# Splitting the negated row maxima of a two-layer cross-attention on GpSimd instead of VectorE

## The chip, the core and the metric

The kernel runs on one core of one Trainium2 chip. The metric is the time of one execution on the device in microseconds. TensorE multiplies matrices, VectorE and ScalarE work on tiles in SBUF and PSUM, GpSimd works on tiles in SBUF, and SyncE issues the DMAs. Each engine takes its own instructions in order; semaphores join them.

## The reference

Two cross-attention layers over 4 batches of 1024 tokens, 16 heads each, all in float32. Layer 0 (heads of 64) is a layer norm, projections of `h = layernorm(x)` and of the context, then

```python
attn = jnp.einsum('bihd,bjhd->bhij', Q, K)
attn = jax.nn.softmax(attn, axis=-1) * scale
vals = jnp.einsum('bhij,bjhd->bihd', attn, V).reshape(B, NQ, INNER)
x = x + vals @ Wo + bo
```

Its scores are not scaled ahead of the softmax, so the kernel subtracts a maximum of each row. Layer 1 (heads of 32) is an RMS norm, a rotary embedding and an L2 normalisation of q and k, a softmax over bounded logits (no maximum is needed), and again a projection and a residual.

## The kernel before, in words

A **turn** is a batch, a layer and a group of heads: two heads of 64 in layer 0 (8 turns a batch), four of 32 in layer 1 (4 turns). A turn has two halves of 512 query tokens. `PLAN` is a list of steps, 4 for a half of layer 0 and 8 for one of layer 1. A step of layer 0 makes the scores of two key tiles of 128, their exponentials (ScalarE), the running sum of the exponentials (VectorE, `added`, L904) and the product with the values (TensorE, `attend`, L721). Beside that it does other work that the plan lists by hand (`layer0_beside`, `layer1_beside`): projections of the next turns, output projections, and the row maxima of layer-0 halves to come. All engines walk the same plan through `run` (L532), each with its own order inside a step; VectorE uses `on_vector` (L268), the others the default of `run`.

**The row maxima.** For a half, TensorE makes eight tiles of plain scores (`rowmax` of TensorE, L668), in two banks of `work`, the only three-bank PSUM buffer for everything beside the attention. VectorE reduces each to one negated maximum per row and head (L883, `tile_max`), which frees the banks. After the eighth, always the last tile maximum of step 1 of a layer-0 half, or of a step in the last layer-1 turn, VectorE takes the minimum over the two halves of the keys (L887, `neg`, 128x8), copies it to bfloat16 (L889) and subtracts that copy from the float32 value for a second bfloat16 part (L891). The two parts lie in `neg_max` in columns 0, 64 and 1, 65 of each tile. There are 64 such completions in the run. Entry `T`, in the next step, has TensorE multiply `neg_max` by an identity (L769) to turn the parts into rows; ScalarE copies them to `shift` (L847), which joins the scores as a fourth product with ones.

**Around it in a steady half of layer 0.** Behind L891 VectorE makes `q_low` or `k_low` (L978, from PSUM and SBUF), normalises the last half's output (`o_sum`, L910, both inputs in SBUF, waits for a DMA of `recip`), reduces the first tile maximum of step 2 (L883) and adds the step's two exponentials (L904, both inputs in SBUF). On TensorE L721 is followed by an output projection (`out`, L793), which claims one of the banks that the tile maximum reads, and then by `T`.

**GpSimd** does the rest of the rotary work for each `kr` and `qr` entry (`finish_rotation`: a power L1028, an addition L1030, a multiplication L1033), the inverse root of the norms (L1049), and the bias addition (L1041, after a DMA of `resid`). Turn 7 of a batch, first half, has `kr` of turn 8 in step 1 and again in step 2; it is the only completion of row maxima whose step has such an entry. In `on_vector` the last tile maximum of a step stands ahead of the step's last entry if that is a `q`, `k`, `kT` or `qT`, and behind all entries if not, so behind this `kr`. VectorE's part of `kr` is five operations ending with L969.

Of the kernel before, what the change touches and what calls it, by code (L numbers as in the profile page):

```python
# [10 lines left out]
ALU = mybir.AluOpType  # L11
ACT = mybir.ActivationFunctionType
AX = mybir.AxisListType

B, S, D, DC = 4, 1024, 512, 384
P = 128
TT = S // P
HALF = 512
HT = HALF // P
XC, CC = D // P, DC // P  # L20
HEADS = 16
D0, D1 = 64, D // HEADS
G0, G1 = P // D0, P // D1
# [347 lines left out]
def max_no(t, n):  # L371

    b, _, p = TURN[t]
    return b * 2 * TURNS0 + ORDER.index((p, n)) + 1


def norm_no(which, half):
    b, l = which
    return 4 * b + 2 * l + half + 1


def build(nc, rows, x, ctx_in, wq0, wk0, wv0, wo0, bo, gamma, beta, norm_w, wq1, wkv1, wout1,
# [16 lines left out]
    def tiles_of(half):  # L399
        return slice(half * HT, (half + 1) * HT)  # L400

    with ExitStack() as ctx:
        def sb(name, shape, dt=F32, scope=ctx):
            return scope.enter_context(nc.sbuf_tensor(name, shape, dt))

        def sem(name):
            return ctx.enter_context(nc.semaphore(name))
# [30 lines left out]
        den_t = sb("den_t", [P, G1, HT])  # L438
        recip_t = sb("recip_t", [P, G1, HT])
        tile_max = sb("tile_max", [P, HT, G0, 2])  # L440
        neg = sb("neg", [P, HT, G0])
        neg_max = sb("neg_max", [P, HT, P], BF16)
        ident_b = sb("ident_b", [P, P], BF16)
        shift = [sb(f"shift{i}", [P, S], BF16) for i in range(2)]
# [21 lines left out]
        consts_ok = sem("consts_ok")  # L466
# [14 lines left out]
        act_freed = sem("act_freed")  # L481
        dve_freed = sem("dve_freed")
        high_ok = sem("high_ok")
        neg_step = sem("neg_step")
        neg_max_ok = sem("neg_max_ok")
        scores_ok = sem("scores_ok")
# [41 lines left out]
        def maxima_banks(e):  # L528

            return work[:, 0:2, :] if e.banks[0] < BANKS else scores[:, e.banks[0] - BANKS:e.banks[1] - BANKS + 1, :]  # L530

        def run(rowmax, scored, blocks, entry, order=lambda st: (st.first + st.early, st.fill + st.rest)):  # L532

            for at, st in enumerate(PLAN):
                after = PLAN[at + 1] if at + 1 < len(PLAN) else None
                if after is not None and not st.late:
                    for kt in after.kts:
                        scored(after.t, after.n, kt)
                ahead, beside = order(st)
                for e in ahead:  # L540
                    (rowmax if e.kind == "R" else entry)(e)
                for kt in st.kts:
                    blocks(st.t, st.n, kt)
                for e in beside:
                    (rowmax if e.kind == "R" else entry)(e)
                if after is not None and st.late:
                    for kt in after.kts:
                        scored(after.t, after.n, kt)
# [328 lines left out]
        def _(dve):  # L877
            def rowmax(e):
                half, n, qt = e.i
                if (n, qt) == (0, 0) and (e.t, half) != (0, 0):  # L880
                    dve.wait_ge(neg_max_ok, max_no(e.t, half) - 1)
                dve.wait_ge(work_full, e.full)
                dve.tensor_reduce(tile_max[:, qt, :, n:n + 1], maxima_banks(e), AX.X, ALU.max, negate=True).then_inc(dve_freed, 1)  # L883
                if (n, qt) == (1, HT - 1):
                    dve.wait_ge(dve_freed, e.dve)
                    no = 2 * max_no(e.t, half)
                    dve.tensor_reduce(neg[:, :, :], tile_max[:, :, :, :], AX.X, ALU.min).then_inc(neg_step, 1)  # L887
                    dve.wait_ge(neg_step, no - 1)
                    dve.tensor_copy(neg_max[:, :, 0:D0 + 1:D0], neg[:, :, :]).then_inc(neg_step, 1)  # L889
                    dve.wait_ge(neg_step, no)  # L890
                    dve.tensor_tensor(neg_max[:, :, 1:D0 + 2:D0], neg[:, :, :], neg_max[:, :, 0:D0 + 1:D0], ALU.subtract).then_inc(neg_max_ok, 1)  # L891

            def added(t, n, kt):
                if kt == 0 or kt > last_sum(t):
# [123 lines left out]
            dve.wait_ge(ident_in, 16)  # L1018
            dve.tensor_copy(ident_b[:, :], ident[:, :]).then_inc(consts_ok, 1)
            run(rowmax, lambda t, n, kt: None, added, entry, on_vector)  # L1020

        @block.gpsimd
        def _(pool):
            def finish_rotation(e):
                which, no, ts = "kq".index(e.kind[0]), e.rope, tiles_of(e.i)
                vec = raw[which][:, ts, :, :]
                pool.wait_ge(sumsq_ok, no)
                pool.tensor_tensor(inv[no % 2][:, :], sumsq[no % 2][:, :], power[:, :], ALU.pow).then_inc(turn_step, 1)  # L1028
                pool.wait_ge(dve_freed, e.dve)
                pool.tensor_tensor(vec, vec, turned[no % 2][:, :, :, :], ALU.add).then_inc(turn_step, 1)  # L1030
                pool.wait_ge(turn_step, 2 * no)
                vec = vec.rearrange("p t h d -> p (t h) d")
                pool.tensor_tensor(vec, vec, inv[no % 2][:, :].unsqueeze(2).broadcast_to([P, HT * G1, D1]), ALU.mult).then_inc(scaled_ok, 1)  # L1033

            def add_bias(b, half):
                ts = tiles_of(half)
                if b == 0:
                    pool.wait_ge(bias_in, 16)
                    pool.wait_ge(xn_ok, norm_no((0, 0), 1))
                pool.wait_ge(resid_in[half], 16 * (b + 1))  # L1040
                pool.tensor_tensor(resid[:, ts, :], resid[:, ts, :], bo_all[:, :].unsqueeze(1).broadcast_to([P, HT, D]), ALU.add).then_inc(bias_ok, 1)  # L1041

            def entry(e):
                if e.kind in ("kr", "qr"):
                    finish_rotation(e)
                elif e.kind == "norm_a":
                    ts = tiles_of(e.i)
                    pool.wait_ge(var_ok, norm_no(e.t, e.i))
                    pool.tensor_tensor(rstd[:, ts], var_eps[:, ts], power[:, 0:HT], ALU.pow).then_inc(rstd_ok, 1)  # L1049
                elif e.kind == "add_bias":  # L1050
                    add_bias(e.t, e.i)
                elif e.kind == "swap":
                    add_bias(e.t, e.i)

            pool.memset(power[:, :], -0.5).then_inc(power_ok, 1)
            pool.wait_ge(power_ok, 1)
            run(lambda e: None, lambda t, n, kt: None, lambda t, n, kt: None, entry)


# [37 lines left out]
```

## Time and profile before

| | us |
|---|---|
| median of three runs | 3179.01 |
| lowest, highest | 3171.63, 3180.96 |
| the profiled execution, its own time | 3179.22 |
| its span, first to last instruction | 3177.4 |
| granted TensorE clock, mean | 0.996 |

The profiled execution has its time beside its span: the instructions fill 3177.4 us of 3179.22. In the timeline a row is one instruction or several of the same line merged: start, duration (of all merged), engine, line, operation, what it writes and reads, and the count; in brackets the idle time of its engine ahead of it and what ended it. PEld is the weight load of TensorE, which can run ahead of the matmul that needs it. The ends of matmuls are modelled, so distances between starts are safer than ends.

### The profile page before, as it was taken

The page shows a single profiled execution, that of the slowest core. Times are in us where ns is not written, and L with a number is a line of the kernel's source. Part 1 is how long each engine was busy: PE and PEld are TensorE (multiplying, and loading weights), DVE is VectorE, ACT ScalarE, POOL GpSimd, SP SyncE. Part 2 cuts the span into 40 slices and gives each one's busy share as a digit, 9 for nine tenths or more (in the row PEclk, how much of TensorE's full clock was granted, in tenths as well). Part 3 has the DMA queues.
Part 4 walks back from the last instruction along what each step waited for, and adds up shares of the span by engine and source line. Part 5 has one row for each costly group of instructions (what it writes and reads, how often), then busy time and mean ns, then how long its engine had stood idle before and what let it go on. Part 6 is the DMA issues. An engine that isn't in the chain of part 4 may idle for free.

```text
span 3177.4 us, 70528 instructions
## 1 busy us (share of the span) xinstructions
PE 3042.6 (96%) x30408; PEld 1482.9 (47%) x30408; DVE 2297.7 (72%) x2683; ACT 1395.4 (44%) x1497; POOL 488.0 (15%) x221
## 2 busy tenths in 40 slices
PE   7999998999999999999999999999999999999998
PEld 4444445554444444555444444455534444445553
DVE  5777777787677777678667777768866777776867
ACT  3333333556433333356643333335563333334565
POOL 1000003450000000245000000125401000013540
PEclk9999999999999999999999999999999999999999
DMA  3000100211210101020121010102112010100001
GB/s 118 19 26 22 26 23 21 57 27 39 63 39 22 26 22 26 16 60 23 42 72 26 22 26 22 29 14 61 28 36 79 22 26 22 26 22 20 22 16 38
DMA packets 178444, 107.12 MB, mean 34 GB/s; under 512 B 81501, under 2 KB 147165, under 8 KB 178137
## 3 DMA queue, kind: packets, MB, share of 16 engines
q1 hardware_dynamic: 178136, 102.60, 12.3%
q8 instruction: 245, 4.01, 0.5%
q14 instruction: 63, 0.51, 0.1%
HBM read 93.12 MB, written 9.42 MB: 32 GB/s over the span
## 4 chain that ended last, share of the span: by engine, by line
PE 80%; DVE 11%; issue 3%; ACT 3%; DMA 3%; SPq 0%; POOL 0%; DVEq 0%; ACTq 0%
PE scores L709 18%; PE o_acc L721 17%; PE work L748 12%; PE work L742 12%; PE work L793 10%; PE work L668 5%; DVE acc L904 3%; DVE tile_max L883 3%; PE work L780 3%; ACT probs L829 1%; DVE o_sum L910 1%; PE work L774 1%; PE scores L702 1%; PE work L784 1%; DMA recip<-rows_dram 1%
## 5 line engine op out<-in xcount | busy, mean ns | idle before, releaser
L829 ACT ACTIVATE probs<-scores 128x1024 f32<-128x1024 f32 (+1 forms) x744 | 934.3, 1290 | 449.7 <-PE scores L709 434.4
L883 DVE TENSOR_REDUCE tile_max<-work 128x2 f32<-128x1024 f32 x500 | 611.4, 1223 | 436.1 <-PE work L668 436.1
L904 DVE TENSOR_TENSOR acc<-acc,probs 128x1024 f32<-128x1024 f32 (+1 forms) x544 | 857.9, 1577 | 31.2 <-ACT probs L829 6.9
L721 PE MATMUL o_acc<-probs,v_tok 128*64 128x512 f32 (+1 forms) x4096 | 769.4, 605 | 0.2 <-ACT probs L825 0.2
L1028 POOL TENSOR_TENSOR inv<-sumsq,power 128x16 f32<-128x16 f32 x64 | 186.2, 2909 | 1956.0 <-DVE sumsq L966 1956.0
L793 PE MATMUL work<-wo,o_sum 128*32 128x512 f32 (+1 forms) x2072 | 399.4, 600 | 59.5 <-issue 27.8
L709 PE MATMUL scores<-q_high,k_high 64*128 64x512 f32 (+1 forms) x1952 | 370.0, 492 | 0.8 <-ACT probs L829 0.8
L721 PEld LDWEIGHTS o_acc<-probs,v_tok 128*64 128x64 f32 (+1 forms) x4096 | 164.5, 122 | 324.7 <-issue 315.5
L988 DVE TENSOR_TENSOR resid<-work,resid 128x512 f32<-128x512 f32 x384 | 261.5, 685 | 70.0 <-PE work L793 69.9
L668 PE MATMUL work<-k_high,q_high 64*128 64x512 f32 x1000 | 267.6, 532 | 31.5 <-DVE tile_max L883 22.2
L709 PE MATMUL scores<-q_low,k_high 64*128 64x512 f32 (+1 forms) x1952 | 296.9, 392 | 0.0
L709 PE MATMUL scores<-q_high,k_low 64*128 64x512 f32 (+1 forms) x1952 | 294.7, 390 | 0.0
L748 PEld LDWEIGHTS work<-wv,cT 128*64 128x64 f32 (+2 forms) x6000 | 258.4, 125 | 55.5 <-issue 54.8
L748 PE MATMUL work<-wv,cT 128*64 128x128 f32 (+2 forms) x6000 | 276.8, 274 | 0.0
L793 PEld LDWEIGHTS work<-wo,o_sum 128*32 128x32 f32 (+1 forms) x2072 | 99.0, 122 | 312.1 <-issue 159.6
L742 PE MATMUL work<-hT,wq 128*64 128x512 f32 (+2 forms) x1144 | 232.1, 592 | 2.0 <-ACT hT L870 2.0
L844 ACT ACTIVATE q_high<-work 128x512 fp32r<-128x512 f32 x96 | 57.5, 599 | 326.4 <-PE work L742 294.5
L709 PE MATMUL scores<-shift,ones_b 64*128 64x512 bf16 x1024 | 200.6, 387 | 0.0
L904 DVE TENSOR_TENSOR acc<-probs 128x1024 f32<-128x1024 f32 (+1 forms) x96 | 157.6, 1642 | 58.3 <-ACT probs L829 44.9
L668 PEld LDWEIGHTS work<-k_high,q_high 64*128 64x128 f32 x1000 | 96.5, 189 | 204.7 <-issue 92.5
L709 PEld LDWEIGHTS scores<-q_high,k_high 64*128 64x128 f32 (+1 forms) x1952 | 145.0, 187 | 82.5 <-issue 65.0
L742 PE MATMUL work<-cT,wk 128*64 128x512 f32 (+2 forms) x852 | 176.9, 593 | 1.4 <-ACT cT L863 1.4
(89 smaller groups left out, 2565.4 us busy)
## 6 DMA issues: line engine op xcount, KB each, us to landing
recip<-rows_dram SPq DMA_DIRECT2D x380, 64.0 KB, 2.2
stage<-in_x_dram SPq DMA_DIRECT2D x8, 1024.0 KB, 7.1
wq<-in_L_xattn_Wq_dram SPq DMA_DIRECT2D x32, 256.0 KB, 2.9
resid<-in_x_dram SPq DMA_DIRECT2D x8, 1024.0 KB, 5.2
wo<-in_L_xattn_Wo_dram SPq DMA_DIRECT2D x32, 256.0 KB, 2.8
out_dram<-resid SPq DMA_DIRECT2D x7, 1024.0 KB, 4.3
wk<-in_L_xattn_Wk_dram SPq DMA_DIRECT2D x32, 192.0 KB, 2.5
wv<-in_L_xattn_Wv_dram SPq DMA_DIRECT2D x32, 192.0 KB, 2.6
```

The costliest lines, as they stand in the source:

```text
L668: mm = pe.matmul(maxima_banks(e)[:, h, :], high["q", par][r, tile(half * HT + qt)], high["k", par][r, tokens(n)], start=True, stop=True)
L709: mm = pe.matmul(scores[:, first + h, :], k_rows, qq[r, tokens(n)], start=(i == 0), stop=(i == len(products) - 1))
L721: mm = pe.matmul(o_acc[h * d:(h + 1) * d, :], v_tok[par][:, kt, h * d:(h + 1) * d], probs[:, unit_slot(t, n, kt, h // 2), h % 2, :], start ...
L742: mm = pe.matmul(w[r, :], wt[:, c, r], src[:, c, tokens(e.i)], start=(c == 0), stop=(c == n_c - 1))
L748: mm = pe.matmul(w[r, tile(j)], src[:, c, part(HT * e.i + j, r)], wt[:, c, :], start=(c == 0), stop=(c == n_c - 1))
L780: mm = pe.matmul(w[h * d:(h + 1) * d, :], ones[l][:, 0:d], acc[buffer_of(e.t, e.i)][:, h, :], start=True, stop=(l == 0))
L793: mm = pe.matmul(w[r, :], o_sum[buffer_of(e.t, n)][:, part(e.i % HT, r)], wo[par][:, :], start=True, stop=True)
L829: act.activation(block_probs(t, n, kt), scores[:, 2 * (no % 2):2 * (no % 2) + g, :], ACT.Exp, scale=(1.0, float(D1) ** 0.5 / QK_SCALE ** 2 ...
L883: dve.tensor_reduce(tile_max[:, qt, :, n:n + 1], maxima_banks(e), AX.X, ALU.max, negate=True).then_inc(dve_freed, 1)
L904: dve.tensor_tensor(a, block_probs(t, n, 0) if kt == 1 else a, block_probs(t, n, kt), ALU.add).then_inc(add_ok, units)
L988: dve.tensor_tensor(resid[:, e.i, :], w, resid[:, e.i, :], ALU.add).then_inc(dve_freed, 1)
L1028: pool.tensor_tensor(inv[no % 2][:, :], sumsq[no % 2][:, :], power[:, :], ALU.pow).then_inc(turn_step, 1)
```

## The change

The minimum over the tile maxima stays on VectorE, which writes it into one of two buffers `neg0`, `neg1` in turn and raises a new semaphore `neg_ok`. GpSimd makes the bfloat16 copy and the difference, in its own walk through the plan, which now has VectorE's order. VectorE waits for the difference of two completions before, instead of one before, where it overwrites `neg`. GpSimd also waits once for the constants at the start, since VectorE clears `neg_max` there.

```diff
-        neg = sb("neg", [P, HT, G0])
+        neg = [sb(f"neg{i}", [P, HT, G0]) for i in range(2)]
...
+        neg_ok = sem("neg_ok")
...
-                if (n, qt) == (0, 0) and (e.t, half) != (0, 0):
-                    dve.wait_ge(neg_max_ok, max_no(e.t, half) - 1)
+                no = max_no(e.t, half)
+                if (n, qt) == (0, 0) and no > 1:
+                    dve.wait_ge(neg_ok, no - 1)
                 dve.wait_ge(work_full, e.full)
                 dve.tensor_reduce(tile_max[:, qt, :, n:n + 1], maxima_banks(e), AX.X, ALU.max, negate=True).then_inc(dve_freed, 1)
                 if (n, qt) == (1, HT - 1):
                     dve.wait_ge(dve_freed, e.dve)
-                    no = 2 * max_no(e.t, half)
-                    dve.tensor_reduce(neg[:, :, :], tile_max[:, :, :, :], AX.X, ALU.min).then_inc(neg_step, 1)
-                    dve.wait_ge(neg_step, no - 1)
-                    dve.tensor_copy(neg_max[:, :, 0:D0 + 1:D0], neg[:, :, :]).then_inc(neg_step, 1)
-                    dve.wait_ge(neg_step, no)
-                    dve.tensor_tensor(neg_max[:, :, 1:D0 + 2:D0], neg[:, :, :], neg_max[:, :, 0:D0 + 1:D0], ALU.subtract).then_inc(neg_max_ok, 1)
+                    if no > 2:
+                        dve.wait_ge(neg_max_ok, no - 2)
+                    dve.tensor_reduce(neg[no % 2][:, :, :], tile_max[:, :, :, :], AX.X, ALU.min).then_inc(neg_ok, 1)
...
         def _(pool):
+            def rowmax(e):
+
+                half, n, qt = e.i
+                if (n, qt) != (1, HT - 1):
+                    return
+                no = max_no(e.t, half)
+                pool.wait_ge(neg_ok, no)
+                pool.tensor_copy(neg_max[:, :, 0:D0 + 1:D0], neg[no % 2][:, :, :]).then_inc(neg_step, 1)
+                pool.wait_ge(neg_step, no)
+                pool.tensor_tensor(neg_max[:, :, 1:D0 + 2:D0], neg[no % 2][:, :, :], neg_max[:, :, 0:D0 + 1:D0], ALU.subtract).then_inc(neg_max_ok, 1)
...
             pool.wait_ge(power_ok, 1)
-            run(lambda e: None, lambda t, n, kt: None, lambda t, n, kt: None, entry)
+            pool.wait_ge(consts_ok, 1)
+            run(rowmax, lambda t, n, kt: None, lambda t, n, kt: None, entry, on_vector)
```

## Rows read from the trace of the kernel before

**Rows 1.** The page: busy time and share of each engine; chain by engine.
```profile
PE 3042.6 (96%) x30408; PEld 1482.9 (47%) x30408; DVE 2297.7 (72%) x2683; ACT 1395.4 (44%) x1497; POOL 488.0 (15%) x221
PE 80%; DVE 11%; issue 3%; ACT 3%; DMA 3%; SPq 0%; POOL 0%; DVEq 0%; ACTq 0%
```
**Rows 2.** The waits: who waited for whom, total us, times, longest us.
```profile
PE work L793 <- DVE tile_max L883: 25.0, 57, 1.6
DVE o_sum L910 <- DMA recip<-rows_dram: 39.2, 22, 4.9
```
**Rows 3.** The timeline of all engines around one steady completion, 417.9 to 422.
```profile
417.92 0.17 DVE L887 TENSOR_REDUCE neg<-tile_max 128x8 f32<-128x16 f32 x1
...
418.35 0.20 DVE L891 TENSOR_TENSOR neg_max<-neg,neg_max 128x8 bf16<-128x8 f32 x1
418.44 0.68 DVE L978 TENSOR_TENSOR q_low<-work,q_high 128x512 fp32r<-128x512 f32 x1
...
418.64 1.94 PE L721 MATMUL o_acc<-probs,v_tok 128*64 128x512 f32 x8
...
419.04 0.68 DVE L910 TENSOR_TENSOR o_sum<-o_sum,recip 128x512 f32<-128x512 f32 x1
...
419.64 1.22 DVE L883 TENSOR_REDUCE tile_max<-work 128x2 f32<-128x1024 f32 x1
...
420.90 1.08 PE L793 MATMUL work<-wo,o_sum 128*64 128x512 f32 x4 [0.33 <-DVE tile_max L883]
...
421.81 0.39 PE L769 MATMUL work<-ident_b,neg_max 128*64 128x128 bf16 x8
```
**Rows 4.** The same timeline one half earlier, at a step without a completion.
```profile
401.28 1.94 PE L721 MATMUL o_acc<-probs,v_tok 128*64 128x512 f32 x8
...
403.05 1.03 PE L793 MATMUL work<-wo,o_sum 128*64 128x512 f32 x4
```
**Rows 5.** The timeline of PE: first and last steady completion of the run.
```profile
106.01 0.65 PE L793 MATMUL work<-wo,o_sum 128*64 128x512 f32 x2 [0.34 <-DVE tile_max L883]
...
2809.09 0.65 PE L793 MATMUL work<-wo,o_sum 128*64 128x512 f32 x2 [0.34 <-DVE tile_max L883]
```
**Rows 6.** The timeline at a turn 7, first half: rotation and completion together, 477 to 486.
```profile
477.51 0.17 DVE L966 TENSOR_SCALAR sumsq<-sumsq 128x16 f32<-128x16 f32 x1
477.59 0.68 DVE L967 TENSOR_TENSOR raw_k<-work,cos 128x512 f32<-128x512 f32 x1
...
477.76 2.91 POOL L1028 TENSOR_TENSOR inv<-sumsq,power 128x16 f32<-128x16 f32 x1 [443.47 <-DVE sumsq L966]
...
480.62 0.69 DVE L910 TENSOR_TENSOR o_sum<-o_sum,recip 128x512 f32<-128x512 f32 x1
480.64 1.79 POOL L1030 TENSOR_TENSOR raw_k<-raw_k,turned 128x512 f32<-128x512 f32 x1
...
482.35 3.21 DVE L904 TENSOR_TENSOR acc<-acc,probs 128x1024 f32<-128x1024 f32 x2
...
482.51 1.97 POOL L1033 TENSOR_TENSOR raw_k<-raw_k,inv 128x512 f32<-128x512 f32 x1
483.40 0.39 PE L769 MATMUL work<-ident_b,neg_max 128*64 128x128 bf16 x8
```
**Rows 7.** The lines by themselves: count, least/median/greatest ns, first and last start.
```profile
L904 DVE TENSOR_TENSOR acc<-acc,probs x544: 1160/1225/3447, 69.9 to 3161.5; 128x1024 f32<-128x1024 f32 x128, 128x2048 f32<-128x2048 f32 x54
...
L1030 POOL TENSOR_TENSOR raw_k<-raw_k,turned x32: 1267/1642/2337, 480.6 to 3059.9; 128x512 f32<-128x512 f32 x32
...
L1041 POOL TENSOR_TENSOR resid<-resid,bo_all x8: 4526/4534/4560, 25.3 to 2453.7; 128x2048 f32<-128x2048 f32 x8
...
L1049 POOL TENSOR_TENSOR rstd<-var_eps,power x16: 1012/1020/3029, 10.4 to 2951.9; 128x4 f32<-128x4 f32 x16
...
L883 DVE TENSOR_REDUCE tile_max<-work x500: 1161/1225/1226, 64.4 to 2867.2; 128x2 f32<-128x1024 f32 x167
```
**Rows 8.** The timeline of POOL at the start of the run.
```profile
0.73 0.11 POOL L1055 MEMSET power<- 128x16 f32 x1 [0.29 <-POOLq L1081]
```

## The prediction

> **What bounds the kernel now.** I read the page first: TensorE is busy for 96% of the span and holds 80% of the chain that ended last, VectorE is busy for 72% and holds 11% [rows 1]. So a microsecond taken from VectorE counts only where TensorE waits for it. The waits come next: the output projection L793 waited 25.0 us in 57 cases for a tile maximum of VectorE [rows 2]. Then the timeline shows where. In a steady half of layer 0, right after a completion of row maxima, VectorE has a backlog: `neg`, its two splits, `q_low`, `o_sum` and the tile maximum follow without idle time, the last ends at 419.64 + 1.22 = 420.86, and L793 starts at 420.90 [rows 3]. It claims a bank that this tile maximum reads. From the start of L721 to that of L793 it is 420.90 - 418.64 = 2.26 us; at a step without a completion it is 403.05 - 401.28 = 1.77 us [rows 4]. TensorE loses 0.49 us here, and VectorE's backlog is the whole cause.
>
> **How often.** Going through the 64 completions one by one, 50 show this pattern with an idle time of about 0.34 us at L793; the first and the last are in [rows 5] (three of the 50 lose about 0.6 us). The other 14: one is at 1075 us, where `o_sum` waited for its DMA; four fall in turn 7, first half (480, 1266, 2054 and 2839 us), with `o_sum` and no `low` operation behind L891; four are in the half after it, where `o_sum` waits for its DMA as well (such waits make the 39.2 us in 22 cases of [rows 2]); three are in layer 1, where `T` comes over 7 us later; two are at the start. In these 14 I count no gain.
>
> **What the removal gives.** L887 starts at 417.92 and `q_low` at 418.44, 0.52 us later, the two splits and their semaphore waits between them [rows 3]. Without them `q_low` follows L887 directly. For that distance I take L966 to L967, also a 0.17 us operation with an independent one behind it: 477.59 - 477.51 = 0.08 us [rows 6]. So 0.44 us leaves VectorE's backlog. The tile maximum then ends at 420.42, L793 starts 1.82 us after L721, still at or above the natural 1.77 us: nothing else is late before the 0.44 us is used up. Upper bound 50 x 0.44 = 22.0 us.
>
> **What the addition costs in the steady halves.** GpSimd is idle there. A wait of GpSimd on VectorE ends fast: L966 ends at 477.68, L1028 starts at 477.76, 0.08 us later [rows 6]. No row has GpSimd on 128x8 with a copy or a difference. Below stands the memset, 0.11 us [rows 8]; above stands L1049 on 128x4, 1.02 us, but that is a power [rows 7]. Nearer in kind are the additions: 1.27 us at 512 elements and 4.53 us at 2048 at best [rows 7], that is 2.12 ns an element and 0.18 us fixed, so 0.2 us for 8 elements. I take 0.2 us for each of the two, because that line is of the same operation, and keep 0.11 and 1.02 for the range. Counted from the start of L887, the copy runs from 0.25 to 0.45, the difference (0.08 us between them) from 0.53 to 0.73. `T` needs the result where TensorE gets there: 421.81 - 417.92 = 3.89, 3.45 after the gain. Slack 2.7 us, and even with 1.02 us each it is enough. So the slower GpSimd is hidden under `q_low`, `o_sum`, the tile maximum and L793.
>
> What may not be hidden is a collision between the engines. `o_sum` would start at 0.60 + 0.08 = 0.68 after L887, while the difference still runs until 0.73. Rows show that VectorE and GpSimd do hold each other up: the two `acc` of turn 7 take 3.21 us with the multiplication of GpSimd beside them, where two alone take about 2.5 (median 1.225 each), and L1030 beside `o_sum` takes 1.79 against 1.27 us at best [rows 6, 7]. Operations that read PSUM don't: the tile maximum never took over 1.226 us in 500 [rows 7]. I take 0.03 us lost per completion, most of a 0.05 us overlap. Gain 50 x 0.41 = 20.5 us.
>
> The Trainium skill states this as a rule (SBUF — State Buffer, "Who interferes with whom"): a VectorE instruction with two SBUF inputs contends with a GpSimd instruction that reads SBUF, and the one that came second waits for all of the other. By that rule the loss is the full overlap, 0.05 us, and the gain 50 x 0.39 = 19.5 us; the rows above on `acc` and the tile maximum agree with it in kind.
>
> **What moves in turn 7, first half.** Here `kr` stands in step 1 ahead of the last row maxima in the plan's order, so GpSimd now has L1028, L1030 and L1033 ahead of the two splits, and they end at 482.51 + 1.97 = 484.48 [rows 6]. Before, `T` ran at 483.40, with its parts long ready. Behind L1033 the copy and the difference need 0.2 + 0.08 + 0.2 us, and the second `acc`, which L1033 held up, now stands against them: it takes its 1.2 us (less 0.1 that it gains) before one of the two, wherever it cuts in. The parts are ready at about 484.48 + 0.5 + 1.1 = 486.1, `T` at 2.7 us later than before. TensorE waits there with everything behind it: the projection of the second `kr`, whose squares feed VectorE and GpSimd in turn, so nothing behind it catches up. Four batches: 4 x 2.7 = 10.8 us lost. Bounds: 1.7 us each without the collision (6.8 us), 4.2 us each with small operations of 1.02 us (17 us). `o_sum` gains little here, since L1028 runs until 480.67.
>
> **Other moves, at nothing.** The bias addition of batch 0 now waits on GpSimd for the first completion at 47 us; its readers L988 start after 100 us. Later bias additions stand at 840 and 880 us, away from completions at 808, 854 and 888. The wait for the constants ends with the first microseconds, its first user L1049 starts at 10.4 us [rows 7]. The waits on `neg_ok` and on the difference of two completions before are met long ahead. No DMA moves; SyncE's queue is untouched. ScalarE's `shift` follows `T` and is needed only by the next half's scores.
>
> **Sum.** Against the profiled execution: 3179.2 - 20.5 + 10.8 = 3169.5 us. The median of the three runs, 3179.0, is 0.2 us below that execution, so I say 3169.3 us, 0.31% less. 0.3% (9.5 us) is about what a measurement of this kernel can tell from no change.
>
> **Rivals.**
> - *The stall in turn 7 is small.* GpSimd goes straight from L1033 into the copy and the difference and VectorE takes its turn after them: 6.8 us lost, 22 gained, 3164 us. For it: successive GpSimd operations start without a gap. Against it: `acc` has been waiting longer. 0.15.
> - *`o_sum` is held up in each steady half.* The copy takes 0.3 us and the difference too; the difference then starts at 0.63, just ahead of `o_sum` at 0.68, and holds it to 0.93. Of 0.44 only 0.19 is left: -9.5 + 10.8 = +1.3, 3180 us. It decides only if the copy ends between 0.45 and 0.60; a longer copy lets `o_sum` in first. The rule of the Trainium skill's page SBUF — State Buffer ("Who interferes with whom") is the one by which this full hold would occur. 0.17.
> - *The small operations cost what L1049 costs.* At 1.02 us the copy itself holds `o_sum` from 0.68 to 1.27, 0.59 us against a gain of 0.44: 50 x 0.15 = 7.5 us more, and 17 us in turn 7: 3203 us, slower. It decides from a copy of about 0.87 us. Against it: L1049 is a power, and 16 elements of it take 2.91 us [rows 6], so most of its time goes by elements. 0.07.
> - *The time taken from VectorE does nothing*, because L793 finds another wait (the `recip` DMA behind `o_sum`, as at 1075 us): +10.8, 3190 us. Against it: in the steady halves VectorE had no idle time ahead of `o_sum`, so the DMA had landed. 0.05.
>
> **Chances.** The forecast has 0.56, and straddles the bound of 0.3%: half of it is faster, half the same. With the first rival faster has 0.28 + 0.16, with the second same has 0.28 + 0.16, slower 0.12. The range runs from 3162 (both bounds good, and a little run-to-run spread) to 3183 (the second rival with spread), leaving out about 0.15.
>
> **What would show it.** Right: L793 <- tile maximum in the waits falls from 25 us to about 4; at a steady completion `q_low` starts 0.08 us after L887 and L721 to L793 is 1.82 us; the POOL operations last about 0.2 us; in the four turns 7 `T` waits for GpSimd some 2 to 3 us, a new row of 7 to 12 us in the waits. Wrong: `o_sum` over 0.75 us long in steady halves, small POOL operations of 0.5 us or more, or no wait of `T` in turn 7.

## The result and the profile after

The changed kernel takes 0.9946 of the time before, with an interval of 0.9934 to 0.9959 (medians 3158.97 us of 7 runs against 3173.74 us of 7). Measured again among the experiments it is 0.9948 (0.9935 to 0.9960). The ratio makes it 17 us faster (the two medians are 14.8 us apart), where 9.7 us were forecast, and 0.9946 of the 3179.0 us that the forecast started from is 3161.8 us, just under its range of 3162 to 3183. The profiled execution has a span of 3155.9 us.

The waits of the changed kernel (engine and line, waited for; total us, times, longest us), with [rows 2] as their counterpart:

```profile
POOL neg_max L1030 <- DVE neg L890: 1736.9, 60, 76.4
...
PE work L794 <- issue: 21.5, 24, 2.3
...
PE work L770 <- POOL neg_max L1032: 7.7, 4, 2.3
PE work L794 <- DVE tile_max L885: 6.3, 10, 1.1
```

L794 is the output projection that was L793. Its wait for a tile maximum fell from 25.0 us in 57 cases to 6.3 us in 10. In its place stands a new row, four waits of `T` (L770) for GpSimd, 7.7 us.

The timeline of the changed kernel at the same steady completion as [rows 3]:

```profile
415.97 0.17 DVE L890 TENSOR_REDUCE neg<-tile_max 128x8 f32<-128x16 f32 x1
416.06 0.69 DVE L977 TENSOR_TENSOR q_low<-work,q_high 128x512 fp32r<-128x512 f32 x1
...
416.21 0.22 POOL L1030 CAST neg_max<-neg 128x8 bf16<-128x8 f32 x1 [32.87 <-DVE neg L890]
416.51 0.24 POOL L1032 TENSOR_TENSOR neg_max<-neg,neg_max 128x8 bf16<-128x8 f32 x1
416.66 0.68 DVE L909 TENSOR_TENSOR o_sum<-o_sum,recip 128x512 f32<-128x512 f32 x1
416.68 1.94 PE L722 MATMUL o_acc<-probs,v_tok 128*64 128x512 f32 x8
...
417.26 1.22 DVE L885 TENSOR_REDUCE tile_max<-work 128x2 f32<-128x1024 f32 x1
...
418.39 2.54 DVE L903 TENSOR_TENSOR acc<-acc,probs 128x1024 f32<-128x1024 f32 x2
418.53 1.08 PE L794 MATMUL work<-wo,o_sum 128*64 128x512 f32 x4
...
419.44 0.39 PE L770 MATMUL work<-ident_b,neg_max 128*64 128x128 bf16 x8
```

`q_low` starts 0.09 us behind the minimum (0.52 before), the copy and the difference take 0.22 and 0.24 us on GpSimd beside it, and `o_sum` keeps its 0.68 us. From L722 to L794 it is 1.85 us, where it was 2.26 before and 1.77 at a step without a completion.

The same at turn 7, first half, with [rows 6] as counterpart. There L721, which [rows 6] leave out, started at 480.56 (first line, kernel before):

```profile
480.56 1.94 PE L721 MATMUL o_acc<-probs,v_tok 128*64 128x512 f32 x8
```
```profile
474.98 2.91 POOL L1038 TENSOR_TENSOR inv<-sumsq,power 128x16 f32<-128x16 f32 x1 [29.27 <-DVE sumsq L965]
...
477.41 0.68 DVE L909 TENSOR_TENSOR o_sum<-o_sum,recip 128x512 f32<-128x512 f32 x1
...
477.77 1.94 PE L722 MATMUL o_acc<-probs,v_tok 128*64 128x512 f32 x8
477.86 1.36 POOL L1040 TENSOR_TENSOR raw_k<-raw_k,turned 128x512 f32<-128x512 f32 x1
...
479.14 3.20 DVE L903 TENSOR_TENSOR acc<-acc,probs 128x1024 f32<-128x1024 f32 x2
479.30 1.97 POOL L1043 TENSOR_TENSOR raw_k<-raw_k,inv 128x512 f32<-128x512 f32 x1
...
481.21 1.21 POOL L1030 CAST neg_max<-neg 128x8 bf16<-128x8 f32 x1
...
482.50 0.23 POOL L1032 TENSOR_TENSOR neg_max<-neg,neg_max 128x8 bf16<-128x8 f32 x1
482.88 0.41 PE L770 MATMUL work<-ident_b,neg_max 128*64 128x128 bf16 x8 [2.31 <-POOL neg_max L1032]
```

The copy comes only behind the rotation and takes 1.21 us in place of 0.22, because it meets the second `acc`. TensorE stands still for 2.31 us. From the start of L722 to that of `T` it is 5.11 us in all four batches, against 2.84 in all four of the profile before (483.40 - 480.56): 2.27 us each, 9.1 us in all. The wait row says 7.7 us and not 4 x 2.31, since in one of the four L722 ran at half clock and took up 1.5 us of what would have been idle time.

### The profile page after: what moved, and what is told of

Same layout as the page of the kernel before. It is cut to its first block, busy times and chain, and to the rows that moved or that the text cites. A ratio compares the mean times of both kernels' runs of the same rounds, so it can differ in the third digit from the quotient of the medians.

```text
span 3155.9 us, 70590 instructions
## 1 busy us (share of the span) xinstructions
PE 3038.5 (96%) x30408; PEld 1484.1 (47%) x30408; DVE 2275.2 (72%) x2555; ACT 1395.2 (44%) x1497; POOL 532.1 (17%) x349
## 4 chain that ended last, share of the span: by engine, by line
PE 83%; DVE 8%; issue 3%; ACT 3%; DMA 2%; POOL 1%; SPq 0%; DVEq 0%; ACTq 0%
PE o_acc L722 19%; PE scores L710 18%; PE work L749 13%; PE work L743 12%; PE work L794 10%; PE work L669 5%; DVE acc L903 3%; PE work L781 3%; ACT probs L830 1%; DVE tile_max L885 1%; PE work L775 1%; PE scores L703 1%; PE work L785 1%; DVE stats L920 1%; DMA rows_dram<-recip_t 1%
## 5 line engine op out<-in xcount | busy, mean ns | idle before, releaser
L722 PE MATMUL o_acc<-probs,v_tok 128*64 128x512 f32 (+1 forms) x4096 | 769.3, 605 | 0.0
L794 PE MATMUL work<-wo,o_sum 128*32 128x512 f32 (+1 forms) x2072 | 398.5, 598 | 34.6 <-issue 21.5
L1030 POOL CAST neg_max<-neg 128x8 bf16<-128x8 f32 x64 | 24.1, 377 | 1736.9 <-DVE neg L890 1736.9
L722 PEld LDWEIGHTS o_acc<-probs,v_tok 128*64 128x64 f32 (+1 forms) x4096 | 164.4, 122 | 324.2 <-issue 315.3
L1038 POOL TENSOR_TENSOR inv<-sumsq,power 128x16 f32<-128x16 f32 x64 | 186.2, 2909 | 495.7 <-DVE sumsq L965 495.7
L794 PEld LDWEIGHTS work<-wo,o_sum 128*32 128x32 f32 (+1 forms) x2072 | 99.5, 122 | 281.2 <-issue 152.8
```

What stands on the lines that cost most here:

```text
L722: mm = pe.matmul(o_acc[h * d:(h + 1) * d, :], v_tok[par][:, kt, h * d:(h + 1) * d], probs[:, unit_slot(t, n, kt, h // 2), h % 2, :], start ...
L794: mm = pe.matmul(w[r, :], o_sum[buffer_of(e.t, n)][:, part(e.i % HT, r)], wo[par][:, :], start=True, stop=True)
```

## The experiments

Each ran beside the kernel before on the same chip. "Ratio" is to the kernel before, with a 95% interval; microseconds behind a ratio are that share of 3175 us.

**Two executions of one program.** The kernel before, unchanged.

> The kernel before, unchanged, timed against itself, to see what two profiled executions of one program differ in. The changed kernel was measured at 0.9946 of before (0.9934 to 0.9959), 17 us; the steps that I can name in the two traces make 21.6 us gained in steady halves and 9.0 us lost in turn 7, first half, so 12.6 us. Theory A, the other 4 to 9 us are chance (landings of the recip DMA, pieces at the lower clock): ratio 1.000 within 0.002, and an instruction by instruction comparison of this trace with the first one shows single steps of 0.5 to 2 us at L793 ahead of which TensorE waits for o_sum's DMA. Theory B, those steps come from the change: the DMA waits of this trace are the same as in the first one within 1 us (PE L793 'issue' 27.8 us, VectorE o_sum 39.2 us).

Ratio 0.9998 (0.9989 to 1.0008). The span of its profiled execution is 3173.9 us, 3.5 us under that of the first profile. Single distances from L721 to L793 differ by 0.3 to 0.8 us where `o_sum` waits for `recip`. Its waits show how far such rows go without any change:

```profile
DVE o_sum L910 <- DMA recip<-rows_dram: 32.2, 18, 4.8
...
PE work L793 <- DVE tile_max L883: 24.3, 57, 1.3
PE work L793 <- issue: 22.3, 25, 2.0
```

The first profile had 39.2 us for `o_sum` and 27.8 us of "issue" at L793, the changed kernel 33.5 and 21.5. So differences of that size come without any change (theory A); the wait for the tile maximum is another matter, it stays at 24 to 25 us.

**The splits ahead of the rotation on GpSimd.**

```diff
-            run(rowmax, ..., entry, on_vector)
+            run(rowmax, ..., entry, lambda st: (on_vector(st)[0], st.rest + st.fill))
```

> The changed kernel, but in each step GpSimd takes the two splits ahead of the rotation entries. Main theory (TensorE loses 2.3 us in each turn 7, first half, because GpSimd comes to the splits only behind L1038, L1040 and L1043): no wait of T for GpSimd is left, the time is 4 x 2.3 = 9 us under the changed kernel, ratio to before about 0.9917 (3148 against 3174 us). Rival (the stall only takes the place of other waits, the DMA wait of the next half shrinks as much): ratio 0.994 to 0.996, as the changed kernel. Rival (the rotation, now 3 us later, is itself waited for): a new wait of TensorE at the transposes L775, ratio above 0.9946.

Ratio 0.9927 (0.9914 to 0.9941), 3151.8 us. No wait of `T` for GpSimd is left, and the rotation, now behind the splits, is waited for by nobody. GpSimd's timeline at turn 7:

```profile
477.62 0.61 POOL L1030 CAST neg_max<-neg 128x8 bf16<-128x8 f32 x1 [31.86 <-DVE neg L890]
478.32 0.23 POOL L1032 TENSOR_TENSOR neg_max<-neg,neg_max 128x8 bf16<-128x8 f32 x1
478.48 2.91 POOL L1038 TENSOR_TENSOR inv<-sumsq,power 128x16 f32<-128x16 f32 x1
```

The parts are ready 4.2 us earlier than in the changed kernel's timeline above (478.55 against 482.73, with the two timelines within 0.1 us of each other here). The step from 0.9948 to 0.9927 is 6.7 us; 9 were expected, and the intervals are 4 us wide to either side.

**Only turn 7 on GpSimd.**

```diff
+                    if no % 16 != 15:
+                        ... # the copy and the difference on VectorE
...
                 no = max_no(e.t, half)
+                if no % 16 != 15:
+                    return
                 pool.wait_ge(neg_ok, no)
```

> Only the four completions in turn 7, first half, are split on GpSimd, behind the rotation; the other 60 on VectorE, as before. Main theory: this is the loss alone, 4 x 2.3 = 9 us, ratio 1.0029 (1.002 to 1.004). Rival (part of the stall is given back in the next half, 0.2 to 0.8 us each, which the two traces show at L793): 4 x 1.7 = 7 us, 1.002. Rival (no loss): 1.000.

Ratio 1.0028 (1.0017 to 1.0039), 8.9 us slower. From L722 to `T` it is 5.11 us in each of the four. That the time fits 4 x 2.27 = 9.1 us is partly luck. In three of the four in the profile L722 ran at half clock, and TensorE's idle time ahead of `T` is 2.31 us once and 0.62 us three times, 4.2 us in all; the rest goes with a lower clock of TensorE in this version (last section). The rival by which the next half gives part of the stall back isn't needed, since the kernel before, run again, had the same shorter waits there, but its 1.002 lies inside the interval too.

**All but turn 7 on GpSimd** (the same edit with `== 15`).

> The changed kernel with the four completions of turn 7, first half, split on VectorE again. Main theory: the gain alone, 50 x 0.43 = 21.6 us and no stall, ratio 0.9932 (0.9915 to 0.994). If it equals the version with the splits ahead of the rotation on GpSimd, VectorE's 0.44 us in turn 7 are worth nothing. Rival (gain 17 us from something other than the tile maxima): L794's idle time behind the tile maximum stays above 20 us.

Ratio 0.9930 (0.9916 to 0.9944). L794 waits for the tile maximum 7.4 us in 12 cases. The time can't be told from that of the version with the splits first. In the traces `T` comes 0.2 us later here (2.84 us behind L722 at full clock, against 2.63 there), so what GpSimd takes from VectorE in turn 7 is worth some 0.8 us in all, which the times don't resolve.

**The changed kernel again.**

> The changed kernel, unchanged, to size it again. From the parts measured one by one (splits on GpSimd in all but turn 7 alone: 0.9930; in turn 7, first half, alone: 1.0028) the sum is 0.9958. Additive parts: ratio 0.995 to 0.9965, 3160 to 3162 us beside 3175. If it comes out at 0.9946 or less again, the two parts are not additive and something of the stall is given back when the steady halves are faster.

Ratio 0.9948 (0.9935 to 0.9960). The two parts (all but turn 7, only turn 7) sum to 0.9958, within its interval but near the end of it. A second measurement of the first part (0.9918, below) brings the sum to 0.9952.

**Both engines split.** GpSimd as in the changed kernel, and VectorE does the same two operations at the old place into a tile that nobody reads.

```diff
                     dve.tensor_reduce(neg[no % 2][:, :, :], tile_max[:, :, :, :], AX.X, ALU.min).then_inc(neg_ok, 1)
+                    dve.wait_ge(neg_ok, no)
+                    dve.tensor_copy(spare[:, :, 0:D0 + 1:D0], neg[no % 2][:, :, :]).then_inc(spare_step, 1)
+                    dve.wait_ge(spare_step, no)
+                    dve.tensor_tensor(spare[:, :, 1:D0 + 2:D0], neg[no % 2][:, :, :], spare[:, :, 0:D0 + 1:D0], ALU.subtract)
```

> The changed kernel with VectorE doing both small operations as well, at their old place, into a spare tile that nobody reads: GpSimd's part is as in the changed kernel, VectorE's time as before. Main theory (the gain is VectorE's 0.44 us ahead of the tile maximum in 50 steady halves and nothing else): the gain is gone and the stall of turn 7 stays, ratio 1.003 (1.002 to 1.004). Rival (the gain came from GpSimd's new order, its bias addition of batch 0 or the waits on neg_ok): ratio stays under 1.

Ratio 1.0034 (1.0021 to 1.0047), 10.8 us slower. So the gain comes from VectorE's time ahead of the tile maximum, and not from GpSimd's new order, its bias addition or the waits on `neg_ok`. Its waits:

```profile
PE work L796 <- DVE tile_max L887: 23.5, 57, 1.4
PE work L796 <- issue: 23.0, 25, 2.3
...
PE work L772 <- POOL neg_max L1038: 7.3, 4, 2.5
```

The wait for the tile maximum is back. In turn 7 `T` comes 5.5 us behind L724 (the line of L721 here), 2.7 more than before, and 4 x 2.7 = 10.8 us. That the time is just this is partly luck, as in only turn 7: the wait row has 7.3 us, and the clock was lower here too. This is the 2.7 us of the prediction: with VectorE's splits in place `o_sum` isn't moved forward, and GpSimd's addition takes 1.79 us as before.

**A long operation on GpSimd ahead of the splits.**

```diff
                 pool.wait_ge(neg_ok, no)
+                pool.tensor_tensor(idle[1][:, :], idle[0][:, :], idle[0][:, :], ALU.add)
```

> The changed kernel with an addition of 128x256 on GpSimd ahead of each pair of splits (0.7 us by the 1.27 us at 512 and 4.53 us at 2048), both inputs in SBUF, results unused. It runs from 0.25 to about 0.95 us behind L890, over the start of o_sum at 0.69. Theory A (such an operation holds VectorE's operation with two SBUF inputs up until it ends): o_sum starts or ends 0.2 to 0.25 us later, the tile maximum too, half of the gain is lost, 50 x 0.2 = 10 us over the changed kernel, 0.9990. Theory B (it is held up only in part, or not at all): o_sum stays at 0.69 us, ratio as the changed kernel plus 4 x 0.7 = 3 us in turn 7, 0.997.

Ratio 0.9978 (0.9969 to 0.9988), 9.5 us over the changed kernel. Theory A's distance of 10 us fits, but its 0.9990 lies outside the interval and theory B's 0.997 inside, so the time doesn't decide. The timeline does:

```profile
414.57 0.68 DVE L979 TENSOR_TENSOR q_low<-work,q_high 128x512 fp32r<-128x512 f32 x1
414.73 0.61 POOL L1032 TENSOR_TENSOR idle<-idle 128x256 f32<-128x256 f32 x1 [31.89 <-DVE neg L892]
415.17 0.72 DVE L911 TENSOR_TENSOR o_sum<-o_sum,recip 128x512 f32<-128x512 f32 x1
415.29 0.69 POOL L1033 CAST neg_max<-neg 128x8 bf16<-128x8 f32 x1
```

`o_sum` starts at 415.17 with the addition running until 415.34, 0.17 us of overlap, and takes 0.72 us in place of 0.68: 0.04 us lost. The copy behind it takes 0.69 us in place of 0.22, since now VectorE was first. L724 to L796 is 1.89 us against 1.85. So 50 x 0.04 = 2 us, and in turn 7 `T` comes 0.55 us later than in the changed kernel, 2.2 us. Some 5 us of the 9.5 are in neither. They go with TensorE's clock: the 12 executions here have a mean granted clock of 0.9933, the 12 of the changed kernel 0.9955, and by the slope in the last section (2.5 us for each 0.001) that is 5 to 6 us.

The small loss doesn't show that VectorE is held up only in part. Other places of the traces have longer overlaps, such as this one in layer 1 of the changed kernel:

```profile
640.24 2.98 POOL L1043 TENSOR_TENSOR raw_k<-raw_k,inv 128x512 f32<-128x512 f32 x1
...
642.23 1.53 DVE L909 TENSOR_TENSOR o_sum<-o_sum,recip 128x512 f32<-128x512 f32 x1
```

`o_sum` met 0.99 us of the multiplication and took 0.85 us longer than its 0.68. Wherever an `o_sum` or `acc` met more than 0.16 us of an addition or multiplication of GpSimd, 47 to 104 places in each of the twelve traces, it lost that overlap less 0.12 to 0.17 us (0.13 in the median). The 0.17 us here lose 0.04, and the 0.09 us of the difference in the changed kernel nothing.

**VectorE relieved of the minimum too.** On top of the splits-first version; GpSimd copies the maxima of the first 512 keys as `neg`, so the minimum over the two halves of the keys is left out.

```diff
-                    dve.tensor_reduce(neg[no % 2][:, :, :], tile_max[:, :, :, :], AX.X, ALU.min).then_inc(neg_ok, 1)
...
+                pool.wait_ge(dve_freed, e.dve)
+                pool.tensor_copy(neg[no % 2][:, :, :], tile_max[:, :, :, 0]).then_inc(neg_ok, 1)
```

> The version with the splits first on GpSimd, and VectorE relieved of its third small operation too: GpSimd copies the negated maxima of the first 512 keys as neg, and the minimum over the two halves of the keys is left out, so only times are read. VectorE gets 0.2 us more. Main theory (the natural distance of L722 to L794 is 1.77 us and 1.85 are reached, so VectorE no longer bounds): 50 x 0.05 to 0.08 = 2.5 to 4 us, ratio 0.9915 to 0.992 against 0.9927. Rival (VectorE still bounds): 50 x 0.2 = 10 us, 0.9895.

Ratio 0.9903 (0.9890 to 0.9916). L722 to L794 is 1.767 us in the median of the steady halves, the natural distance:

```profile
415.63 0.68 DVE L904 TENSOR_TENSOR o_sum<-o_sum,recip 128x512 f32<-128x512 f32 x1
415.74 0.67 POOL L1029 TENSOR_TENSOR neg_max<-neg,neg_max 128x8 bf16<-128x8 f32 x1
415.85 1.94 PE L722 MATMUL o_acc<-probs,v_tok 128*64 128x512 f32 x8
...
416.23 1.22 DVE L885 TENSOR_REDUCE tile_max<-work 128x2 f32<-128x1024 f32 x1
...
417.62 1.03 PE L794 MATMUL work<-wo,o_sum 128*64 128x512 f32 x4
```

VectorE no longer bounds there. The 0.24% less than the splits-first version is 7.6 us, more than the 4 of 50 x 0.08, with overlapping intervals (0.9914 is in both). The rival's 0.9895 lies inside the interval too; it is the timeline that refutes it, with 0.08 us gained by TensorE for the 0.2 us taken from VectorE.

**The whole completion later, on VectorE.** Without GpSimd: minimum, copy and difference stay on VectorE, behind the first tile maximum of step 2 and ahead of its `acc`, with two buffers for `tile_max`.

```diff
-                if (n, qt) == (1, HT - 1):
-                    ...
+                finish()          # the three operations of the completion that is pending
+                if (n, qt) == (1, HT - 1):
+                    pending.append(e)
...
             def added(t, n, kt):
+                finish()
```

> No operation on GpSimd: the kernel before, but VectorE makes the minimum, the copy and the difference behind the first tile maximum of the next step and ahead of its acc, with two buffers for the tile maxima. Main theory (TensorE loses only what VectorE does between the last tile maximum of step 1 and the first of step 2): L721 to L793 is 1.77 us in the steady halves, 50 x 0.51 = 25 us gained; the parts are ready 2.95 us behind the old start of L887, T gets there at 2.95 to 3.4 us, so no wait of T or up to 0.1 us each; no stall in turn 7. Ratio 0.992 (0.991 to 0.9935). Rival (VectorE's total work bounds, the acc and resid that are now later are waited for): new waits of TensorE on resid or of ScalarE on acc, ratio 0.996 to 1.000.

Ratio 0.9920 (0.9905 to 0.9935), 3150.1 us.

```profile
416.32 1.22 DVE L901 TENSOR_REDUCE tile_max<-work 128x2 f32<-128x1024 f32 x1
417.45 0.16 DVE L889 TENSOR_REDUCE neg<-tile_max 128x8 f32<-128x16 f32 x1
...
417.72 1.03 PE L793 MATMUL work<-wo,o_sum 128*64 128x512 f32 x4
417.87 0.20 DVE L893 TENSOR_TENSOR neg_max<-neg,neg_max 128x8 bf16<-128x8 f32 x1
417.96 2.55 DVE L920 TENSOR_TENSOR acc<-acc,probs 128x1024 f32<-128x1024 f32 x2
418.58 0.39 PE L769 MATMUL work<-ident_b,neg_max 128*64 128x128 bf16 x8
```

The parts are ready at 418.07 and `T` follows L793 without idle time. VectorE does all it did before, and TensorE loses nothing in the steady halves: it was the place of the small operations that cost, not VectorE's total. The rival came true in a small way elsewhere. Three waits of `T` for `resid` grew from 1.1 to about 1.6 us each and three of the transposes (L774) from 0.9 to 1.4 us, 3 us in all, and in turn 7 `T` waits 0.1 us.

**All but turn 7 on GpSimd, once more.**

> GpSimd splits in all completions but those of turn 7, first half, again, on the same chip as the deferred version: 0.993 as before. Main theory: the deferred version is 0.08 us faster in each steady half (1.77 against 1.85 us from L721 to L793), 4 us, 0.1%, at the edge of what is seen.

Ratio 0.9918 (0.9904 to 0.9933), 3148.5 us. The three versions that beat the changed kernel and leave nothing out (splits first, all but turn 7, deferred) can't be told apart.

## Why the prediction was wrong, point by point

**What bounds: right.** L793 waited for VectorE's backlog, and the small operations ahead of the tile maximum were paid for one to one: putting them back on VectorE, with all the rest of the change in place, took the gain away (both engines split, 1.0034).

**The gain, "50 x 0.41 = 20.5 us": right in mechanism, too small.** This is one of the two terms that failed. Instruction by instruction, TensorE gains 0.42 us at the median of these places, 21.5 us over the 50 and the one at 1075 us. The 0.03 us that I took off for a collision wasn't there: `o_sum` met 0.09 us of the difference (416.75 - 416.66) and kept its 0.68 us. By time the gain measures 22.2 and 26.0 us (0.9930 and 0.9918 of 3175).

**The copy and the difference, "0.2 us for each of the two": right,** 0.22 and 0.24 us. The line through two additions of other sizes was the right row, L1049 at 1.02 us the wrong one.

**The stall in turn 7, "4 x 2.7 = 10.8 us": too large.** This is the other term that failed, and the step is "`o_sum` gains little here, since L1028 runs until 480.67", with a rotation that ends as late as before. It is 2.27 us each, 9.1 us. `o_sum` started 2.43 us behind the start of the power (477.41 - 474.98), where it was 2.86 us before (480.62 - 477.76), as VectorE no longer had the splits ahead of it. So the addition L1040 met a piece of `o_sum` that was 0.43 us shorter and took 1.36 us against 1.79, and GpSimd ended the rotation 0.43 us sooner. With both engines splitting, `o_sum` was at its old distance again and the stall was the 2.7 us. The mechanism was as told: rotation first, then a copy held up by `acc` (1.21 us), then 2.3 us of idle TensorE.

**The sum.** By the traces it is 21.5 - 9.1 = 12.4 us, 0.9961, where I had 9.7. Measured are 0.9946 and 0.9948, each with its interval ending at 0.9959 or 0.9960. So 3 us of the 7 that were missing are the two terms by their steps. For the rest, the means of all executions on record help (the chips differ, so they are a rough check): 3175.3 us for the kernel before (69), 3159.5 for the changed kernel (12), 3151.4 for the 16 with the gain and no stall (splits first, all but turn 7 twice), 3183.7 for only turn 7 (11). That is a gain of 23.9 us and a loss of 8.4, together 15.5, and 15.8 were measured. So the two parts do add up, and what the steps don't explain lies in the gain, 2 to 3 us more than the 21.5 of the steady places. About 1 us of it goes with the clock (0.9964 in the 16 executions, 0.9959 in the kernel before); the other 1 to 2 us are within the spread and stay open.

**The clock, at nothing.** The sum has no term for TensorE's clock. The stalls brought stretches at half clock behind them, which cost time, and some fell into a stretch that would have cost time without them, which made them cheaper (last section). In the changed kernel the mean granted clock is 0.9955, against 0.9959 before, 1 us by the slope and within the spread.

**The rivals.** The small stall in turn 7 (3164 us) was the nearest in time, but for the wrong reason: `acc` did cut in. The hold of `o_sum` is refuted in the changed kernel, since the copy took 0.22 us and the difference ended 0.09 us into `o_sum`. The mechanism that it names is real: an `o_sum` that met 0.99 us of a multiplication lost 0.85. The rule of the Trainium skill that I set beside it (SBUF — State Buffer, "Who interferes with whom": the second one waits for all of the first) agrees with the trace where VectorE came first (copy 0.69 and 1.21 us in place of 0.22, difference 0.67 in place of 0.24). Where VectorE came second it agrees but for the last 0.13 us of GpSimd's addition or multiplication, which decides in overlaps as short as these, and not at all beside GpSimd's power: `o_sum` met 0.48 us of L1038 in turn 7 and took 0.68 us. The small operations at the price of L1049 are refuted by their rows, and so is the gain that finds another wait.

**The range** was set by these cases and not by the spread of the reference: the median of before fell from 3179.0 us in three runs to 3173.7 in seven. Of the 10.3 us between the forecast of 3169.3 us and the median of 3159.0, 5.3 us lie there. In the chances, the two rivals of 0.15 and 0.17 were both added up as 0.16.

## What to carry to other kernels

Find the waits of the bounding engine first, and then count what the engine it waits for does just ahead of the releasing operation. Here 0.4 us of small operations cost 0.4 us each time, and moving them 2 us later on the same engine was as good as giving them to another. The small operations cost nothing on GpSimd where its queue was idle, and 2.3 us each time where 6 us of rotation stood ahead of them: look for the few places where the queue isn't idle, 4 of 64 here, and put the urgent work first in the order.

## What the runs showed of the hardware

**Two engines on SBUF.** A VectorE operation with both inputs in SBUF (`o_sum`, `acc`) that started beside an addition or multiplication of GpSimd was held until some 0.13 us ahead of the end of that operation, in every trace. Beside GpSimd's power (L1028, L1038) none was held: with 1.8 us of it still to run, `o_sum` took 0.68 us and an `acc` of 128x1024 1.22 us, as they do alone. The other way round, GpSimd's copy waited out VectorE's operation (0.69 and 1.21 us in place of 0.22).

**TensorE's clock.** The granted clock fell to half (1.2 GHz) for stretches of 3.4 us, in a few cases 6.8. In the changed kernel one came right behind a stall; in the version with only turn 7 on GpSimd, one came ahead of it, where TensorE had waited 1.8 us for the tile maximum (us, busy us of PE, PEld, DVE, ACT, POOL, granted clock, then DMA):

```profile
2038.50:2041.00 2.50, 0.19 (x4) 0.05 (x3) 2.44 (x2) 0.00 (x0) 2.26 (x3) 1.00 0.00 0
2042.30:2045.60 3.30, 3.30 (x34) 2.97 (x30) 0.00 (x0) 0.00 (x0) 0.00 (x0) 0.50 0.00 0
2045.70:2049.00 3.30, 2.21 (x18) 1.22 (x18) 2.66 (x6) 2.46 (x3) 1.72 (x1) 1.00 0.20 60
```
```profile
2053.20:2056.60 3.40, 1.60 (x14) 0.76 (x12) 3.33 (x8) 1.94 (x2) 2.92 (x2) 1.00 0.18 57
2056.70:2060.00 3.30, 3.30 (x10) 0.93 (x8) 3.20 (x4) 0.00 (x0) 3.22 (x3) 0.50 0.00 0
```

The second kind comes with and without the stall: a stretch began within 1.2 us of the start of L722 (L721, L724) at 10 of the 20 turns 7 in the five profiles with the stall and at 10 of the 28 in the seven without. The first kind comes with the stall alone: a stretch began 4.9 to 15.6 us behind the start of L722 at 14 of the 20, and between 2 and 30 us behind it at none of the 28.

Both change what a stall costs. Without a stall `T` comes 2.84 us behind L721 at full clock and 4.1 to 4.3 us where L721 ran at half clock. With the stall it comes at 5.11 us either way, so a stall that falls into such a stretch costs 0.8 to 1.0 us and not 2.27. A stretch behind the stall then costs time of its own. Between the two exponentials of ScalarE around `T` there are 9.2 to 9.6 us without a stall at full clock, 11.7 with the stall, and 13.3 to 13.4 where the clock fell right behind it.

The profiles are few, but the executions agree. The mean granted clock is 0.9959 in the 62 executions of the kernel before that have it on record, 0.9942 in the 11 with only turn 7 on GpSimd, 0.9938 in the 6 with both engines splitting and 0.9933 in the 12 with the long operation. In those 62, each 0.001 less goes with 2.5 us more (3170.8 us at 0.998, 3180.2 at 0.994, on average). So some 4 of the 8.9 us of only turn 7 go with the clock. In the 12 executions of the changed kernel it is 0.9955, which can't be told from the kernel before.
